# Converting six weight matrices with one DRAM-to-DRAM transfer each instead of tile by tile through SBUF

## The chip, the cores and the metric

The kernel runs on all 8 cores of one Trainium2 chip. Each core handles one of the eight sequences of the input and does the same work; the cores don't exchange data, and each converts its own copy of all weights. The metric is the device time of the slowest core in microseconds, lower is better.

## The reference

One transformer layer on an input of 8 x 4096 x 1024 float32. A modulation vector is made from `L0_c`, then an attention part and a gated feed-forward part are added to the stream:

```python
mod = (_silu(L0_c) @ L0_wmod).reshape(L0_c.shape[0], 6, 1, -1)
...
h = _layernorm(x, axis=-1) * (1 + ca) + sa
x = x + ga * _L0_attn_ref(h, ...)     # q, k, v, o: 1024x1024; fc: 4096x1024; proj: 1024x4096
h = _layernorm(x, axis=-1) * (1 + cb) + sb
x = x + gb * _L0_ffn_ref(h, w_gate, w_up, w_down)
```

`_L0_attn_ref` holds four projections, an attention over the 16 heads within each position, and a GELU MLP. `_L0_ffn_ref` uses weights quantized to -1, 0 and 1: each of gate, up and down (4 million elements each) is scaled by the mean of its absolute values, rounded and clipped:

```python
scale = 1.0 / jnp.clip(jnp.mean(jnp.abs(w)), 1e-05)
wq = jnp.clip(jnp.round(w * scale), -1.0, 1.0) / scale
```

All weights arrive as float32, and TensorE is to multiply in bfloat16.

## The kernel before

**Preparation.** The kernel first makes bfloat16 copies of all nine weight matrices in DRAM scratch tensors (`scr_q` ... `scr_d`), and then loads weights from these for every chunk. The preparation has three kinds of work.

- The modulation: 24 loads of 1024 KB of `wmod` into two buffers (`prefA`, `prefB`) on SP's queue (L252), each load waiting for the TensorE product that read its buffer before; 768 matmuls (L260); a copy of the result by VectorE (L271) and some small operations.
- Six casts, `prep_cast` (L309 to L321): q, k, v and o (1024 x 1024 each, 8 tiles of 128 x 1024), fc and proj (4 million elements each, 16 tiles of 128 x 2048; `fl` regroups the 128 columns of the tensor to rows of 2048). For each tile GpSimd issues a load from DRAM into the one buffer `prep_b` (L315), the DMA converting float32 to bfloat16 on the way, and SP issues the store from `prep_b` to the scratch tensor (L318). The load waits for the store before it, and the store for its load. `first_dep` chains the matrices one behind the other.
- Three quantizations, `prep_quant` (loads L332 and L382, reduction L336, conversions L385 and L389, stores L392): g, u and d, each read twice, once for the mean of its absolute values, once to convert. g begins when the modulation's product (`ev_mod_mm`) and the last cast are done, u after g, d after u. They use the same two buffers as wmod.

**Queues and dependencies.** The order on every engine is the order in which the operations are written. `Prog.op` turns dependencies into waits on semaphores. Every DMA of one of the two DMA queues (SP's "q", GpSimd's "g") alternates between two semaphores, and also waits until the semaphore's previous DMA has landed, so that at most two DMAs of a queue are in flight. A DMA instruction that waits holds back everything behind it on its engine:

```python
s = pool[self.dma_rr[dma] % len(pool)]
self.dma_rr[dma] += 1
deps = list(deps) + [(s, self.counts[s])]
```

SP's queue holds in this order: 11 loads of constants, the 24 loads of wmod, the 64 stores of the casts, the 48 stores of the quantizations, then for chunk 0 the load of x (L550) and the weight loads (`wload`, L421).

**Main part.** Eight chunks of 512 positions follow, one after the other: two layer norms, q, k, v in two slabs, attention, the o projection, fc and proj (weights from `scr_fc`, `scr_proj`), layer norm, gate and up, the requantization and down. Every weight load names the preparation of its matrix (`prep_done[...]`) as a dependency.

Of the kernel before, what the change touches and what calls it, by code (L numbers as in the profile page):

```python
# [15 lines left out]
D = 1024  # L16
H = 16
HD = 64
INNER = 4096
NCD = D // 128  # L20
NCI = INNER // 128
# [54 lines left out]
def build_nc(ttot=TTOT, chunk=CHUNK, slab=SLAB):  # L76
# [5 lines left out]
    p = Prog()  # L82

    dr = {}
# [44 lines left out]
    scr = {}  # L129
# [69 lines left out]
    prep_b = gfm[:, 0:2048]  # L199
# [24 lines left out]
    for nm in cb:  # L224
        p.op("sync", (lambda nm: lambda s: s.dma_start(out=cb[nm][:], in_=dr[nm]))(nm),
             dma="q")
    ev_const = [("dq0", p.counts["dq0"]), ("dq1", p.counts["dq1"])]

    if DBG and PHASE in (232, 99):
        ev_sent = p.op("vector", lambda v: v.memset(mmin[:, 0:128], 7.0), sig=True)  # L230
        p.op("sync", lambda s: s.dma_start(out=dbg["dbg_sbd"], in_=mmin[:, 0:128]),
             deps=[ev_sent], dma="q")
# [7 lines left out]
    for nm_, dst in (("qb_r", qbb), ("kb_r", kbb), ("vb_r", vbb)):  # L240
        ev_bb = p.op("gpsimd", (lambda nm_, dst: lambda g: g.dma_start(
            out=dst[:], in_=dr[nm_]))(nm_, dst), dma="g")
# [3 lines left out]
                   deps=ev_const, sig=True)  # L246
    ev_mod_mm = None
    wmod_hist = []
    for kc in range(8):
        for part in range(3):  # L250
            buf = prefA if (kc * 3 + part) % 2 == 0 else prefB
            evd = p.op("sync", (lambda kc, part, buf: lambda s: s.dma_start(  # L252
                out=buf[:], in_=dr["wmod"][128 * kc:128 * (kc + 1),
                                           2048 * part:2048 * (part + 1)]))(kc, part, buf),
                deps=(wmod_hist[-2] if len(wmod_hist) >= 2 else None,), dma="q")
            last = None
            for m in range(16):
# [3 lines left out]
                    out=bcp[0][:, mg:mg + 1], lhsT=buf[:, 128 * m:128 * (m + 1)],  # L261
                    rhs=siluc[:, kc:kc + 1],
                    start=(kc == 0 and mg == 0), stop=(kc == 7 and mg == 47)))(m, mg, kc, buf),
                    deps=[evd, ev_silu] + (bank_w("bc0") if (kc == 0 and mg == 0) else []),
                    sig=sig)
                if kc == 7 and mg == 47:
                    ev_mod_mm = last
            wmod_hist.append(last)
    if ev_mod_mm is None:
        ev_mod_mm = wmod_hist[-1]  # L270
    ev_mods = p.op("vector", lambda v: v.tensor_copy(out=mods[:], in_=bcp[0][:, 0:48]),  # L271
                   deps=(ev_mod_mm,), sig=True)
# [3 lines left out]
                  deps=(ev_mods,), sig=True)  # L276
    ev_cb1 = p.op("vector", lambda v: v.tensor_scalar(out=mods[:, 32:40], in0=mods[:, 32:40],
                                                      scalar1=1.0, scalar2=None, op0=ALU.add),
                  deps=(ev_mods,), sig=True)
    ev_g = ev_mods  # L280
    for col in (16, 40):
        ev_s0 = p.op("scalar", (lambda col: lambda s: s.activation(
            out=m8[:], in_=mods[:, col:col + 8], func=AF.Sign))(col),
            deps=(ev_g,), sig=True)
        ev_sq = p.op("vector", lambda v: v.scalar_tensor_tensor(
            out=trA[:, 0:8], in0=m8[:], scalar=1.0, in1=m8[:],
            op0=ALU.mult, op1=ALU.mult), deps=(ev_s0,), sig=True)
        ev_sq2 = p.op("vector", lambda v: v.tensor_scalar(
            out=trA[:, 0:8], in0=trA[:, 0:8], scalar1=-1.0, scalar2=1.0,
            op0=ALU.mult, op1=ALU.add), deps=(ev_sq,), sig=True)  # L290
        ev_sgn = p.op("vector", lambda v: v.tensor_tensor(
            out=m8[:], in0=m8[:], in1=trA[:, 0:8], op=ALU.add),
            deps=(ev_sq2,), sig=True)
        ev_a1 = p.op("vector", (lambda col: lambda v: v.scalar_tensor_tensor(
            out=trA[:, 0:8], in0=mods[:, col:col + 8], scalar=-1.0,
            in1=mods[:, col:col + 8], op0=ALU.mult, op1=ALU.max))(col),
            deps=(ev_g, ev_sgn), sig=True)
        ev_a2 = p.op("vector", lambda v: v.tensor_scalar(
            out=trA[:, 0:8], in0=trA[:, 0:8], scalar1=0.25, scalar2=None,
            op0=ALU.max), deps=(ev_a1,), sig=True)  # L300
        ev_g = p.op("vector", (lambda col: lambda v: v.tensor_tensor(
            out=mods[:, col:col + 8], in0=m8[:], in1=trA[:, 0:8],
            op=ALU.mult))(col), deps=(ev_a2, ev_sgn), sig=True)
    ev_mods_done = p.op("vector", lambda v: v.tensor_copy(out=m8[:], in_=mods[:, 0:8]),
                        deps=(ev_g, ev_ca1, ev_cb1), sig=True)

    prep_done = {}

    def prep_cast(src, dst, nrow128, ncols, first_dep=None):  # L309
        evo = None  # L310
        evi = first_dep
        for r in range(nrow128):
            for c0 in range(0, ncols, 2048):
                cw = min(2048, ncols - c0)
                evi = p.op("gpsimd", (lambda r, c0, cw: lambda g: g.dma_start(  # L315
                    out=prep_b[:, 0:cw], in_=src[128 * r:128 * (r + 1), c0:c0 + cw]))(r, c0, cw),
                    deps=(evo, evi), dma="g")
                evo = p.op("sync", (lambda r, c0, cw: lambda s: s.dma_start(  # L318
                    out=dst[128 * r:128 * (r + 1), c0:c0 + cw], in_=prep_b[:, 0:cw]))(r, c0, cw),
                    deps=(evi,), dma="q")  # L320
        return evo  # L321

    def prep_quant(src, dst, nrow128, ncols, sw_col, first_dep=None):
        nsl = nrow128 * (ncols // 2048)
# [54 lines left out]
        for r in range(nrow128):  # L379
            for c0 in range(0, ncols, 2048):  # L380
# [17 lines left out]

    fl = lambda apx: apx.rearrange("(r c) m -> r (c m)", c=16)
    prep_done["q"] = prep_cast(dr["qT"], scr["q"], NCD, D)  # L400
    prep_done["k"] = prep_cast(dr["kT"], scr["k"], NCD, D, first_dep=prep_done["q"])
    prep_done["v"] = prep_cast(dr["vT"], scr["v"], NCD, D, first_dep=prep_done["k"])
    prep_done["o"] = prep_cast(dr["oT"], scr["o"], NCD, D, first_dep=prep_done["v"])
    prep_done["fc"] = prep_cast(fl(dr["fcB"]), fl(scr["fc"]), NCI * D // 16 // 128, 2048,
                                first_dep=prep_done["o"])
    prep_done["proj"] = prep_cast(fl(dr["projB"]), fl(scr["proj"]),
                                  NCD * INNER // 16 // 128, 2048,
                                  first_dep=prep_done["fc"])
    prep_done["g"] = prep_quant(fl(dr["gB"]), fl(scr["g"]), NCI * D // 16 // 128, 2048, 0,
                                first_dep=[ev_mod_mm, prep_done["proj"]])  # L410
    prep_done["u"] = prep_quant(fl(dr["uB"]), fl(scr["u"]), NCI * D // 16 // 128, 2048, 1,
                                first_dep=[prep_done["g"]])
    prep_done["d"] = prep_quant(fl(dr["dB"]), fl(scr["d"]), NCD * INNER // 16 // 128, 2048, 2,
                                first_dep=[prep_done["u"]])
# [134 lines left out]
    for ci in range(nch):  # L549
        ev_x = p.op("sync", (lambda ci: lambda s: s.dma_start(  # L550
            out=xfm[:], in_=x_src[:, :, ci * chunk:(ci + 1) * chunk]))(ci),
            deps=[ev_store_prev] + ev_x_prev_readers, dma="q")
# [5 lines left out]
        if DBG and ci == 0:  # L558
            p.op("sync", lambda s: s.dma_start(out=dbg["dbg_mask"], in_=cb["mask128"][:]),
                 deps=ev_const, dma="q")  # L560
            p.op("sync", lambda s: s.dma_start(out=dbg["dbg_h"], in_=hfm[:]),
                 deps=evs_h + [("sV", p.counts["sV"]), ("sS", p.counts["sS"])], dma="q")
            p.op("sync", lambda s: s.dma_start(out=dbg["dbg_xn"], in_=mmin[:]),
                 deps=evs_xn, dma="q")
            p.op("sync", lambda s: s.dma_start(out=dbg["dbg_mods"], in_=mods[:]),
                 deps=[ev_mods_done], dma="q")

        if PHLE(1):
            ev_store_prev = p.op("sync", (lambda ci: lambda s: s.dma_start(
                out=out_dst[:, :, ci * chunk:(ci + 1) * chunk], in_=xfm[:]))(ci),  # L570
                deps=evs_xn, dma="q")
# [5 lines left out]
        for si in range(nslab):  # L577
# [4 lines left out]
            for TN in ("q", "k", "v"):  # L582
# [3 lines left out]
                for hb in range(4):  # L586
                    bank = pP[hb % 2]
                    ev_mm = None
                    for hs in range(4):
                        h = hb * 4 + hs  # L590
                        for kc in range(NCD):
# [3 lines left out]
                                             out=bank[0:64, hs * slab:(hs + 1) * slab],  # L595
# [46 lines left out]
            if DBG and ci == 0 and si == 0:  # L642
                p.op("sync", lambda s: s.dma_start(out=dbg["dbg_kq"], in_=khq[:]),
                     deps=dep_kh, dma="q")
# [723 lines left out]
```

How the kernel before makes its waits and increments, by code:

```python
            def run(eng):  # L1284
                waited = {}
                for emit, deps, incs in p.ops[eng_name]:
                    for (s, v) in deps:
                        if waited.get(s, 0) < v:
                            eng.wait_ge(sems[s], v)
                            waited[s] = v
                    inst = emit(eng)
                    if inst is not None:
                        for (s, amt) in incs:
                            inst.then_inc(sems[s], amt)
```

## Time and profile before

| | |
|---|---|
| median of 3 runs | 8901.75 us (8900.06 to 8910.51) |
| profiled execution | 8912.2 us |
| its span, core 4 (slowest) | 8910.7 us |
| spans of the 8 cores | 8828.5 to 8910.7 us |
| busy share of the span | TensorE 55%, VectorE 37%, ScalarE 9%, GpSimd 1% |
| mean granted TensorE clock, core 4 | 0.800 of full |
| first work of chunk 0 | 1313.4 us |

The span runs from the first to the last instruction of a core. Busy time is the time in which an engine executes; waiting and the issuing of DMAs don't count. The share of the DMA engines is a mean over the core's 16. The bytes of a DMA are those that it writes.

### The profile page before, as it was taken

To read this page: it belongs to the slowest core of one execution; us is meant where nothing else is said; L and a number is where in the kernel's file an instruction comes from. 1 tells how busy PE (TensorE), PEld (TensorE's weight loads), DVE (VectorE), ACT (ScalarE), POOL (GpSimd) and SP (SyncE) were. 2 spreads that over 40 slices of the span, in tenths; PEclk is the share of its full clock that TensorE was granted. 3 is DMA by queue.
4 is the path that set the end of the run, shared out by engine and by line. 5 is a ranking of instruction groups with operands and counts; after the bars stand their busy time and mean duration, and the time that the engine had idled before them with its cause. 6 is when DMAs were issued, how large, how long until landed. Compare 5 with 4: busy or idle time off the path is not lost.

```text
span 8910.7 us, 70916 instructions; the slowest of 8 cores (8828.5 to 8910.7 us)
## 1 busy us (share of the span) xinstructions
PE 4871.4 (55%) x23724; PEld 2394.2 (27%) x23948; DVE 3298.8 (37%) x6752; ACT 775.3 (9%) x1053; POOL 104.2 (1%) x167
## 2 busy tenths in 40 slices
PE   7000006566556665665656655665566656657566
PEld 7000003322332233222422233223322332214222
DVE  0003334335432543154324443354415432543244
ACT  0000001010101110110011010101011101100110
POOL 0001100000000000000000000000000000000000
PEclk9999997688668876887778867787688767877678
DMA  4355550133203330233113401332033202331133
GB/s 131 85 122 201 198 198 31 37 75 88 73 22 76 83 95 21 67 75 84 49 37 79 110 29 38 72 85 80 22 76 83 85 30 61 74 91 48 31 78 90
DMA packets 1051312, 692.64 MB, mean 78 GB/s; under 512 B 808144, under 2 KB 939344, under 8 KB 1035600
## 3 DMA queue, kind: packets, MB, share of 16 engines
q1 hardware_dynamic: 1027824, 562.26, 23.8%
q0 software_dynamic: 23136, 125.85, 5.1%
q8 instruction: 202, 3.31, 0.2%
q14 instruction: 150, 1.23, 0.0%
HBM read 646.09 MB, written 67.11 MB: 80 GB/s over the span
## 4 chain that ended last, share of the span: by engine, by line
PE 40%; DMA 26%; DVE 21%; issue 10%; ACT 2%; DVEq 1%; SPq 0%; ACTq 0%; POOLq 0%; POOL 0%
PE pA L594 5%; PE pB L594 4%; PE pB L1072 4%; PE pA L1066 3%; DVE sbd L685 3%; DMA wbigA<-scr_fc 2%; DMA wbigB<-scr_u 2%; PE pB L939 2%; PE pA L939 2%; DVE vtmp L1156 2%; DVE vtmp L497 2%; DMA wbigA<-scr_u 2%; PE pB L919 2%; DMA wbigB<-scr_g 2%; PE bcA L260 2%
## 5 line engine op out<-in xcount | busy, mean ns | idle before, releaser
L356 PE MATMUL bcB<-onecol_f,trA 128*1 128x1 f32 x6 | 0.6, 163 | 980.9 <-DVE prep_r L345 980.9
L948 DVE SCALAR_TENSOR_TENSOR vtmp<-pA,c_projb_f,afm 128x512 f32<-128x512 f32 x32 | 24.0, 751 | 1066.2 <-PE pA L939 1066.2
L447 PE MATMUL bcA<-amid,onescol_b 128*1 128x512 bf16 x256 | 102.9, 575 | 469.5 <-DVE amid L440 469.5
L1088 DVE TENSOR_TENSOR gu<-pB,gt 128x512 f32<-128x512 f32 x256 | 177.0, 692 | 445.7 <-PE pB L1072 445.7
L1066 PE MATMUL pA<-mmin,wbigB 128*128 128x512 bf16 x996 | 254.6, 391 | 147.0 <-DMA wbigB<-scr_g 87.5
L336 DVE TENSOR_REDUCE prep_r<-gfm 128x1 f32<-128x2048 f32 x48 | 109.6, 2286 | 604.5 <-DMA gfm<-gB 521.7
L1066 PE MATMUL pA<-mmin,wbigA 128*128 128x512 bf16 x996 | 253.0, 389 | 126.9 <-DMA wbigA<-scr_g 76.3
L1072 PE MATMUL pB<-mmin,wbigB 128*128 128x512 bf16 x1008 | 254.8, 395 | 72.7 <-DMA wbigB<-scr_u 71.3
L1072 PE MATMUL pB<-mmin,wbigA 128*128 128x512 bf16 x1008 | 254.1, 395 | 54.6 <-DMA wbigA<-scr_u 52.5
L356 PEld LDWEIGHTS bcB<-onecol_f,trA 128*1 128x1 f32 x6 | 0.3, 80 | 981.1 <-issue 981.1
L1086 ACT ACTIVATE sig<-gt 128x512 bf16<-128x512 f32 x256 | 161.1, 629 | 1141.3 <-DVE gt L1083 1141.2
L594 PE MATMUL pA<-mmin,wbigB 128*64 128x256 bf16 x1536 | 229.4, 294 | 38.9 <-ACT mmin L507 38.9
L594 PE MATMUL pA<-mmin,wbigA 128*64 128x256 bf16 x1536 | 226.7, 291 | 38.8 <-ACT mmin L507 38.8
L1083 DVE TENSOR_TENSOR gt<-pA,rsxg_t 128x512 f32<-128x512 f32 x256 | 176.6, 690 | 133.7 <-PE pA L1066 132.5
L1207 PE MATMUL pA<-gfm,wbigA 128*128 128x512 bf16 x504 | 164.2, 446 | 101.4 <-DVE gfm L1159 96.1
L1207 PE MATMUL pA<-gfm,wbigB 128*128 128x512 bf16 x504 | 164.1, 446 | 101.6 <-DVE gfm L1159 96.1
L469 ACT ACTIVATE row<-row,ceps 1x512 f32<-1x512 f32 x32 | 23.0, 720 | 2153.3 <-DVE row L464 2153.1
L594 PE MATMUL pB<-mmin,wbigB 128*64 128x256 bf16 x1536 | 203.7, 276 | 0.0
L594 PE MATMUL pB<-mmin,wbigA 128*64 128x256 bf16 x1536 | 203.7, 276 | 0.0
L626 DVE TENSOR_SCALAR gu<-gt 64x1024 bf16<-64x1024 bf16 x128 | 53.6, 419 | 401.6 <-ACT gt L622 401.6
L919 PE MATMUL pA<-mmin,wbigA 128*128 128x512 bf16 x504 | 146.1, 426 | 100.7 <-DMA wbigA<-scr_fc 63.9
L1156 DVE TENSOR_TENSOR vtmp<-gfm,sxb_t 128x512 int32<-128x512 bf16 x256 | 177.2, 692 | 56.3 <-ACT sxb_t L1129 30.4
(228 smaller groups left out, 9086.3 us busy)
## 6 DMA issues: line engine op xcount, KB each, us to landing
gfm<-gB POOLq DMA_DIRECT2D x32, 1024.0 KB, 6.4
gfm<-uB POOLq DMA_DIRECT2D x32, 1024.0 KB, 6.5
gfm<-dB POOLq DMA_DIRECT2D x32, 1024.0 KB, 6.4
wbigB<-scr_fc SPq DMA_DIRECT2D x128, 256.0 KB, 2.9
wbigA<-scr_fc SPq DMA_DIRECT2D x128, 256.0 KB, 2.9
wbigB<-scr_g SPq DMA_DIRECT2D x128, 256.0 KB, 2.9
wbigA<-scr_u SPq DMA_DIRECT2D x128, 256.0 KB, 2.9
wbigA<-scr_g SPq DMA_DIRECT2D x128, 256.0 KB, 2.9
```

The lines of the kernel that those rows point to most:

```text
L260: last = p.op("tensor", (lambda m, mg, kc, buf: lambda t: t.matmul(out=bcp[0][:, mg:mg + 1], lhsT=buf[:, 128 * m:128 * (m + 1)], rhs=siluc ...
L497: ev1 = p.op("vector", (lambda c, scl, vt: lambda v: v.scalar_tensor_tensor(out=vt[:], in0=src[:, c * chunk:(c + 1) * chunk], scalar=scl, ...
L594: (lambda h, hs, kc, wb, bank, t0, st: lambda t: t.matmul(out=bank[0:64, hs * slab:(hs + 1) * slab], lhsT=wb[:, kc * D + h * 64:kc * D + ( ...
L685: v.scalar_tensor_tensor(out=s_out, in0=s_in, scalar=1.0, in1=m_in, op0=ALU.mult, op1=ALU.mult))(s_in, m_in, s_out),
L919: ev_mm = p.op("tensor", (lambda oc, kc, wb, sl: lambda t: t.matmul(out=pslot(sl), lhsT=wb[:, kc * 128:(kc + 1) * 128], rhs=mmin[:, kc * c ...
L939: ev_mm = p.op("tensor", (lambda oc, kc, wb, sl: lambda t: t.matmul(out=pslot(sl), lhsT=wb[:, kc * 128:(kc + 1) * 128], rhs=gfm[:, kc * ch ...
L1066: ev_mg = p.op("tensor", (lambda oc, kc, wbg_, slg: lambda t: t.matmul(out=pslot(slg), lhsT=wbg_[:, kc * 128:(kc + 1) * 128], rhs=mmin[:, ...
L1072: ev_muu = p.op("tensor", (lambda oc, kc, wbu_, slu: lambda t: t.matmul(out=pslot(slu), lhsT=wbu_[:, kc * 128:(kc + 1) * 128], rhs=mmin[:, ...
L1083: ev_p1 = p.op("vector", (lambda slg, gt: lambda v: v.tensor_tensor(out=gt[:], in0=pslot(slg), in1=rsxg_t[:], op=ALU.mult))(slg, gt), deps ...
L1088: ev_p3 = p.op("vector", (lambda slu, gt, gu: lambda v: v.tensor_tensor(out=gu[:], in0=pslot(slu), in1=gt[:], op=ALU.mult))(slu, gt, gu), ...
L1156: ev_q1 = p.op("vector", (lambda oc: lambda v: v.tensor_tensor(out=qi[:], in0=gfm[:, oc * chunk:(oc + 1) * chunk], in1=sxb2_t[:], op=ALU.m ...
L1207: ev_mm = p.op("tensor", (lambda oc, kc, wb, sl: lambda t: t.matmul(out=pslot(sl), lhsT=wb[:, kc * 128:(kc + 1) * 128], rhs=gfm[:, kc * ch ...
```

## The change

`prep_cast` no longer goes through SBUF. It issues one DMA on GpSimd's queue from the whole float32 matrix to the whole scratch tensor, the DMA converting on the way. The six casts no longer depend on each other; fcB and projB are passed as declared (32768 x 128) and not regrouped. g's quantization no longer names the proj cast as a dependency, only the modulation's product. The rule of the two semaphores of a queue stays for all of them.

```diff
     def prep_cast(src, dst, nrow128, ncols, first_dep=None):
-        evo = None
-        evi = first_dep
-        for r in range(nrow128):
-            for c0 in range(0, ncols, 2048):
-                cw = min(2048, ncols - c0)
-                evi = p.op("gpsimd", (lambda r, c0, cw: lambda g: g.dma_start(
-                    out=prep_b[:, 0:cw], in_=src[128 * r:128 * (r + 1), c0:c0 + cw]))(r, c0, cw),
-                    deps=(evo, evi), dma="g")
-                evo = p.op("sync", (lambda r, c0, cw: lambda s: s.dma_start(
-                    out=dst[128 * r:128 * (r + 1), c0:c0 + cw], in_=prep_b[:, 0:cw]))(r, c0, cw),
-                    deps=(evi,), dma="q")
-        return evo
+        return p.op("gpsimd", lambda g: g.dma_start(out=dst, in_=src),
+                    deps=(first_dep,), dma="g")
...
     prep_done["q"] = prep_cast(dr["qT"], scr["q"], NCD, D)
-    prep_done["k"] = prep_cast(dr["kT"], scr["k"], NCD, D, first_dep=prep_done["q"])
-    prep_done["v"] = prep_cast(dr["vT"], scr["v"], NCD, D, first_dep=prep_done["k"])
-    prep_done["o"] = prep_cast(dr["oT"], scr["o"], NCD, D, first_dep=prep_done["v"])
-    prep_done["fc"] = prep_cast(fl(dr["fcB"]), fl(scr["fc"]), NCI * D // 16 // 128, 2048,
-                                first_dep=prep_done["o"])
-    prep_done["proj"] = prep_cast(fl(dr["projB"]), fl(scr["proj"]),
-                                  NCD * INNER // 16 // 128, 2048,
-                                  first_dep=prep_done["fc"])
+    prep_done["k"] = prep_cast(dr["kT"], scr["k"], NCD, D)
+    prep_done["v"] = prep_cast(dr["vT"], scr["v"], NCD, D)
+    prep_done["o"] = prep_cast(dr["oT"], scr["o"], NCD, D)
+    prep_done["fc"] = prep_cast(dr["fcB"], scr["fc"], NCI * D // 16 // 128, 2048)
+    prep_done["proj"] = prep_cast(dr["projB"], scr["proj"],
+                                  NCD * INNER // 16 // 128, 2048)
     prep_done["g"] = prep_quant(fl(dr["gB"]), fl(scr["g"]), NCI * D // 16 // 128, 2048, 0,
-                                first_dep=[ev_mod_mm, prep_done["proj"]])
+                                first_dep=[ev_mod_mm])
```

## Rows read from the trace of the kernel before

**Rows 1.** The page, part 2: busy tenths in 40 slices of the span.

```profile
PE   7000006566556665665656655665566656657566
...
DVE  0003334335432543154324443354415432543244
...
PEclk9999997688668876887778867787688767877678
DMA  4355550133203330233113401332033202331133
```

**Rows 2.** Windows of core 4: stretch, its length, busy us (x instructions) per engine, granted clock, DMA share, GB/s.

```profile
core 4: us, PE busy (x) PEld busy (x) DVE busy (x) ACT busy (x) POOL busy (x), PEclk, DMA share, GB/s
...
15.40:187.30 171.90, 164.10 (x768) 163.99 (x768) 0.05 (x1) 1.49 (x2) 0.53 (x1) 1.00 0.44 152
187.30:395.70 208.40, 0.00 (x0) 0.00 (x0) 2.61 (x16) 0.42 (x2) 15.82 (x30) 1.00 0.36 76
395.70:673.10 277.40, 0.00 (x0) 0.00 (x0) 0.00 (x0) 0.00 (x0) 16.92 (x33) 1.00 0.51 121
673.10:1302.90 629.80, 2.23 (x12) 1.83 (x12) 232.63 (x162) 0.00 (x0) 68.60 (x96) 1.00 0.56 199
1302.90:2255.90 953.00, 585.66 (x2868) 278.26 (x2896) 382.80 (x821) 97.80 (x132) 0.00 (x0) 0.79 0.26 65
2255.90:8910.70 6654.80, 4119.40 (x20076) 1950.14 (x20272) 2679.97 (x5747) 675.58 (x917) 0.00 (x0) 0.76 0.26 65
```

**Rows 3.** Timeline of GpSimd, SP and VectorE: start, us, instruction, wait before and releaser.

```profile
1.57 0.62 POOL L241 DMA_DIRECT2D qbb<-qb_r  x1 [0.88 <-POOLq L81]
...
5.77 0.54 POOL L315 DMA_DIRECT2D gfm<-qT  x1
181.28 0.53 POOL L315 DMA_DIRECT2D gfm<-qT  x1 [174.97 <-DMA scr_q<-gfm]
...
535.78 0.53 POOL L315 DMA_DIRECT2D gfm<-projB  x1 [7.95 <-DMA scr_fc<-gfm]
...
664.33 0.53 POOL L315 DMA_DIRECT2D gfm<-projB  x1 [8.05 <-DMA scr_proj<-gfm]
673.06 1.05 POOL L332 DMA_DIRECT2D gfm<-gB  x2 [8.21 <-DMA scr_proj<-gfm]
...
1.06 0.40 SPq L225 DMA_DIRECT2D c_ob_f<-ob_f  x1
...
14.30 0.33 SPq L225 DMA_DIRECT2D c_cfm<-cfm  x1
15.43 157.54 SPq L252 DMA_DIRECT2D gfm<-wmod  x24
173.12 51.91 SPq L318 DMA_DIRECT2D scr_q<-gfm  x8
...
541.27 128.87 SPq L318 DMA_DIRECT2D scr_proj<-gfm  x16
...
1302.85 0.38 SPq L550 DMA_DIRECT2D xfm<-x_fm  x1
...
187.25 0.21 DVE L271 COPY mods<-bcA 128x48 f32<-128x48 f32 x1 [185.33 <-PE bcA L260]
...
1313.37 2.29 DVE L440 CAST amid<-xfm 128x4096 bf16<-128x4096 f32 x1 [11.02 <-DMA xfm<-x_fm]
```

**Rows 4.** DMA queues in the casts of k, v and o, 230 to 395 us.

```profile
q0 software_dynamic: 3406, 6.19, 26.4%
q1 hardware_dynamic: 3456, 6.29, 10.1%
```

**Rows 5.** DMA queues in the casts of fcB and projB, 410 to 660 us.

```profile
q0 software_dynamic: 4147, 15.12, 36.0%
q1 hardware_dynamic: 4176, 15.21, 15.0%
```

**Rows 6.** Windows of cores 4 and 5, 686 to 690 us, during the gB loads.

```profile
686.00:690.00 4.00, 0.00 (x0) 0.00 (x0) 0.97 (x1) 0.00 (x0) 0.00 (x0) 1.00 0.98 379
...
core 5: us, PE busy (x) PEld busy (x) DVE busy (x) ACT busy (x) POOL busy (x), PEclk, DMA share, GB/s
686.00:690.00 4.00, 0.00 (x0) 0.00 (x0) 3.11 (x2) 0.00 (x0) 0.60 (x2) 1.00 0.32 68
```

**Rows 7.** DMA queues, 1700 to 1850 us, mostly loads of scr_fc.

```profile
q1 hardware_dynamic: 34320, 10.23, 29.9%
...
wbigA<-scr_fc SPq DMA_DIRECT2D x16, 256.0 KB, 2.9
```

## The prediction

> **What bounds the kernel now.** I read the page's forty slices first. TensorE is busy at the start, then has no digit above 0 until slice 7, while the DMA engines stand at 3 to 5 tenths: a stretch of some 1,100 us in which no engine sets the pace by its own work [rows 1]. The windows cut that stretch by what the code does in it [rows 2]. From 15.4 to 187.3 us TensorE multiplies wmod (164.1 of 171.9 us busy). From 187.3 to 673.1 us nothing computes: the six casts run. From 673.1 to 1302.9 us the three quantizations run, and then come eight chunks of about 951 us each ((8910.7 - 1302.9)/8).
>
> The timeline of the GpSimd and SP queues tells why the casts take so long [rows 3]. GpSimd issues the first qT tile at 5.77 us and the second at 181.28 us. The wait between them, 174.97 us, ends with the first store to scr_q, and that store stands in SP's queue behind all 24 wmod loads, the last of which waits for TensorE. From there on it is a strict alternation through one buffer: load a tile, store it, load the next, 6 to 7 us a pair for the 256 KB tiles and 8.6 us for the 512 KB ones (664.33 is the last of 16 projB tiles, the first was at 535.78: 128.55/15 = 8.57). The first gB load leaves at 673.06 us, released by the last scr_proj store. After it all is a chain: the quantizations, then at 1302.85 us the first x load in SP's queue, then at 1313.37 us the first work of chunk 0. So a microsecond taken from the 673.06 is a microsecond off the end, as long as the wmod product is not what the gB load waits for. It is done when VectorE copies it, at 187.25 us: that is the floor, and 673.1 - 187.3 = 486 us is the most that can be won.
>
> **The change, part by part.** It removes 64 loads on GpSimd's queue and 64 stores on SP's, with their waits, and adds six casting transfers from DRAM to DRAM. They have no dependency of their own. They keep the one that every DMA has, on the completion of the last but one of its queue, so two are in flight: q, v, fc share one semaphore, k, o, proj the other. They are issued from 5.8 us on, and nothing waits for SP any more. The order of gB moves: its first load waits for fc and for the wmod product, its second for proj. Behind these two stand all of GpSimd's quantization loads, and behind those VectorE. So what counts is one time, T, at which proj has landed and the wmod product is done. The saving is 673.1 - T; quantizations and chunks keep their durations, as their instructions and dependencies are the same.
>
> *Bytes.* The casts read 4 x 4.19 + 2 x 16.78 = 50.3 MB as float32 and write 25.2 MB as bfloat16 (the tiles show the written side: 8 x 256 KB and 16 x 512 KB). wmod is 24 x 1024 KB = 25.2 MB beside them.
>
> *The issuing.* 63 waits of some 8 us on GpSimd and as many on SP go. One DMA instruction holds GpSimd for 0.53 us at 128 rows and for 0.62 us at one row [rows 3]: a price per row can't be read from that, and six instructions cost some microseconds at most. Taken as 3 us, hidden behind the transfers before.
>
> *The transfers.* No row shows a DRAM-to-DRAM cast, so I bound it. What the 16 DMA engines do for the casts today, without the gaps, is share times duration [rows 2]: 0.36 x 208.4 + 0.51 x 277.4 = 75.0 + 141.5 = 216.5 us. Their wmod work is 0.44 x 171.9 = 75.6 us, and will now lie beside the casts instead of before them. With the engines kept full, T = 5.8 + 216.5 + 75.6 = 298 us, and 3 us of issue make it 301. This is what it costs if reading and writing take an engine as much as two transfers through SBUF do.
>
> The lower bounds: loads and stores come apart by queue, since the loads are GpSimd's (q0) and the stores SP's (q1). At 256 KB a load tile takes 0.264 x 165 x 16 = 697 engine-us for 3406/144 = 23.7 tiles, 29.5 each, or 230 ns for a row of 1024 elements [rows 4]. At 512 KB it is 0.360 x 250 x 16 = 1440 for 28.8 tiles, 50.0 each, or 391 ns for a row of 2048 [rows 5]; a store there takes 0.150 x 4000 / 29 = 20.7. If the write side hides wholly under the read side, the casts cost the loads alone: (32 x 29.5 + 32 x 50.0)/16 = 159 us, T = 5.8 + 75.6 + 159 = 240 us. If long rows also shed the fixed part (391 - 230 = 161 ns for 1024 elements, 69 ns fixed), it is 12,288 x 0.161/16 = 124 us and T = 205 us. All lie above the floor of 187. The upper ones are rivals, below.
>
> I take 301 us. The engines stood at a share of 0.98 and 379 GB/s only in bursts of a few microseconds, while a neighbouring core was at 68 GB/s in the same four [rows 6]; no row holds a burst rate for long, and now all eight cores cast at once, each writing to HBM half of what it reads. That speaks against the two low ends, which need 16 engines at read rate throughout. Saving: 673.1 - 301 = 372 us.
>
> The Trainium skill, HBM Reference, "Specifications (TRN2)", gives a core 358 GB/s when both cores of a pair stream. Casts and wmod move 50.3 + 25.2 + 25.2 = 100.7 MB over HBM, by that 281 us, so an estimate by the page is T = 287 us and a time of 8516 us. The row of 379 GB/s does not contradict it, since it lasts 4 us and the neighbour stood at 68; no run here shows a long stream yet.
>
> *What else could move.* The constants' loads on SP (1.06 to 14.30 us) and then wmod share the engines with the casts; each constant's load waits for an earlier one, so a few microseconds each, at most some 20 us, inside the range. The 64 stores no longer stand in SP's queue before the quantization's stores, which wait for VectorE anyway: nothing. TensorE's granted clock is 1.00 in every stretch before 1302.9 us and 0.76 to 0.79 after [rows 2]; it idles for over 100 us before chunk 0 in both kernels, so chunk 0 starts from the same state: nothing.
>
> *The sum.* The profiled execution took 8912.2 us (span 8910.7), 10 us over the median of the runs, 8901.75. Less 372 this is 8540 for that execution, and 8901.75 - 372 = 8530 us for a median.
>
> **The rivals.**
>
> *The write side hides* (T from 205 to 265 us). For it: one descriptor stream instead of two. Against it: HBM takes both sides at once. Time 8434 to 8494 us. Chance 0.22.
>
> *The wmod product becomes the late one.* The engines are shared between queues, and a wmod load may stand behind long cast rows; then TensorE waits for wmod until the casts are through. For it: wmod keeps TensorE busy 164.1 of 171.9 us [rows 2], so each load that comes later than its two buffers cover counts. Against: the DMA engines have 0.56 of their time free there. Worst case, the casts first and then the whole wmod stretch: 5.8 + 216.5 + 171.9 = 394 us, saving 279, time 8623 us. Chance 0.08.
>
> *Short rows.* fcB and projB are declared 128 columns wide; the old code regrouped them to rows of 2048 elements before the DMA, the new one hands them over as they are. If the rows stay 128 wide there are 65,536 of them. A row of 256 bytes costs 0.299 x 150 x 16 / 34,320 = 21 ns in the weight loads [rows 7], which would be cheap (86 us in all); with the cast's fixed part, 69 + 161/8 = 89 ns, it is 65,536 x 0.089/16 = 365 us, plus 59 for q, k, v and o: T = 5.8 + 75.6 + 365 + 59 = 506 us, saving 167, time 8735 us. Against it: both sides are contiguous, so nothing forces short rows. Chance 0.08.
>
> *One engine each (slower).* A contiguous block has no partition dimension, and if such a copy is not dealt out over the 16 engines, each of the two lanes runs at one engine's rate: 8 x 29.5 + 8 x 29.5 + 16 x 50.0 = 1272 us, T = 1278 us, 605 us later than now, time 9507 us. It decides from one engine: with two each, the lanes take 636 us, T = 642 us, and the time is still 31 us below the present one. For it: no row shows a DMA without a partition side. Against: the shares reach 0.98 of 16 engines in all others. Chance 0.05. The Trainium skill, DMA: Bandwidth & Descriptors, "Why a DMA increments its semaphore by 16 and not by 1", says that software can split a contiguous single-dimension pattern so that it sprays over the engines; by it this case would not come.
>
> *The casts stay as slow.* For T = 673 us the new transfers would have to read their 50.3 MB at 50.3/667 = 75 GB/s over 16 engines. The fit above gives one engine 4096 bytes in 161 ns, 25 GB/s, and the gB loads reach 379 GB/s on 16 [rows 6]; only some limit of the DRAM-to-DRAM path that no row shows could do it. No change. Chance 0.02.
>
> **How the numbers follow.** Main case 0.55, its own range T from 265 to 335 us, 8494 to 8564 us. Faster by over 0.2% (18 us, about what a measurement of this kernel can tell): 0.55 + 0.22 + 0.08 + 0.08 = 0.93. Same: 0.02. Slower: 0.05. The range reaches down to 8430, the bound where write side and fixed parts vanish, and up to 8640, over the late wmod product; short rows, one engine and no gain stay outside (0.15).
>
> **What the next profile would show.** The first gB load at about 301 us instead of 673.06, released by fc or proj. VectorE's copy of the wmod product not far past 187 us; if it comes at 300 or later, wmod is the late one. The DMA share from 6 us to T near 0.9 or higher: if it is at 1.0 and T near 240, the write side hides; if it is well below 0.9, the engines wait for memory. The quantizations at 630 us and the chunks at 951 us, unchanged. The forecast is wrong if the cast's packets are many and short, if a transfer lands on few engines, or if the quantization's pace depends on something that the casts left behind.

## The result, and the profile after

The changed kernel takes 8634.44 us (median of 9 runs, 8611.91 to 8709.33) against 8904.26 us before (10 runs): a ratio of 0.9707, 95% interval 0.9679 to 0.9736, some 270 us faster. The forecast was faster by 372 us. The direction held, but the median lies 104 us above the forecast of 8530, outside the likeliest case's own range (8494 to 8564), at the upper edge of the full one (8430 to 8640). By the ratio it is 8641 us (8616 to 8667) on the forecast's basis of 8901.75, just past that edge. The case that came is a rival, the late wmod product, which had 8623 us and a chance of 0.08.

The page of the profiled execution (8664.66 us, span 8662.9 on core 0), part 2. Against [rows 1] the empty stretch of TensorE has moved: its 7 tenths come one slice later, and the DMA share of the first slice is 9.

```profile
PE   0700065666566575665566655665666656657566
...
DMA  9555501333033311332033211340133303331134
```

The windows of core 0: stretch, length, busy us (x instructions) per engine, granted clock, DMA share, GB/s.

```profile
5.70:183.00 177.30, 0.00 (x0) 0.00 (x0) 0.00 (x0) 0.00 (x0) 3.13 (x7) 1.00 1.01 110
183.00:242.00 59.00, 0.00 (x0) 0.00 (x0) 0.00 (x0) 1.49 (x2) 0.00 (x0) 1.00 0.95 113
242.00:408.60 166.60, 163.97 (x768) 163.91 (x768) 0.40 (x3) 0.21 (x1) 0.03 (x1) 1.00 0.43 146
408.60:1038.10 629.50, 2.23 (x12) 1.83 (x12) 234.94 (x176) 0.21 (x1) 68.63 (x96) 1.00 0.56 199
1038.10:8662.90 7624.80, 4744.64 (x23168) 2237.97 (x23168) 3066.40 (x6568) 773.32 (x1049) 0.00 (x0) 0.76 0.26 64
```

Against [rows 2]: until 242 us the DMA engines are full and TensorE does nothing at all. The wmod product then takes 166.6 us at a DMA share of 0.43, as it did before at 0.44. The quantizations take 629.5 us (629.8) and the chunks (8662.9 - 1038.1)/8 = 953 us each (951). So everything that the forecast left alone did stay, and the whole error lies ahead of 408.6 us.

The timelines of GpSimd, SP and VectorE: start, us, instruction, wait before and its releaser.

```profile
5.71 0.51 POOL L310 DMA_DIRECT2D scr_q<-qT  x1
...
86.50 0.55 POOL L310 DMA_DIRECT2D scr_proj<-projB  x1 [18.13 <-DMA scr_o<-oT]
408.57 1.08 POOL L322 DMA_DIRECT2D gfm<-gB  x2 [321.52 <-PE bcA L260]
...
6.77 0.33 SPq L225 DMA_DIRECT2D c_ln2b_f<-ln2b_f  x1
...
144.35 0.33 SPq L225 DMA_DIRECT2D c_cfm<-cfm  x1
183.00 211.74 SPq L252 DMA_DIRECT2D gfm<-wmod  x24
...
1038.13 0.38 SPq L538 DMA_DIRECT2D xfm<-x_fm  x1
...
408.09 0.21 DVE L271 COPY mods<-bcA 128x48 f32<-128x48 f32 x1 [406.18 <-PE bcA L260]
```

GpSimd issues its six casts as forecast and waits for nothing of SP's. SP's queue does not run as forecast: c_cfm, issued at 14.30 us in [rows 3], goes out at 144.35 us, and wmod begins at 183.00 us instead of 15.43. The first gB load leaves at 408.57 us, released by the wmod product and not by a cast. Its time against 673.06 is a saving of 264.5 us, which is the measured one (some 270 us) within the scatter of the runs. The DMA queues from 6 to 242 us (name, kind: packets, MB written, share; below, KB and us from issue to landing):

```profile
q0 software_dynamic: 896, 25.17, 97.2%
q1 hardware_dynamic: 1051, 0.99, 2.2%
...
scr_proj<-projB POOLq DMA_DIRECT2D x1, 8192.0 KB, 155.4
...
c_cfm<-cfm SPq DMA_DIRECT2D x1, 4.0 KB, 81.9
```

A transfer of 128 rows shows 144 packets in the kernel before, one of a single row 32. Without 16 for each of the six casts and 32 for vbb, the 896 packets are 768 rows, and 25.17 MB over 768 are 32,768 bytes written: the rows are 64 KB read and 32 KB written, eight times longer than any row of the casts before. A constant of 4 KB takes 82 us to land.

### The profile page after: what moved, and what is told of

Same layout as the page of the kernel before. It is cut to its first block, busy times and chain, and to the rows that moved or that the text cites. A ratio compares the mean times of both kernels' runs of the same rounds, so it can differ in the third digit from the quotient of the medians.

```text
span 8662.9 us, 70774 instructions; the slowest of 8 cores (8566.8 to 8662.9 us)
## 1 busy us (share of the span) xinstructions
PE 4910.8 (57%) x23948; PEld 2403.7 (28%) x23948; DVE 3302.5 (38%) x6752; ACT 775.2 (9%) x1053; POOL 73.6 (1%) x109
## 3 DMA queue, kind: packets, MB, share of 16 engines
q8 instruction: 202, 3.31, 0.2%
## 4 chain that ended last, share of the span: by engine, by line
PE 41%; DMA 22%; DVE 21%; issue 10%; another core or an unknown queue 3%; ACT 2%; DVEq 1%; SPq 0%; ACTq 0%; POOL 0%; POOLq 0%
PE pA L582 5%; PE pB L582 5%; PE pB L1060 3%; PE pA L1054 3%; DVE sbd L673 3%; PE pB L927 2%; DMA wbigA<-scr_u 2%; DVE vtmp L1144 2%; DMA wbigA<-scr_fc 2%; DMA wbigB<-scr_fc 2%; DMA wbigA<-scr_g 2%; DMA wbigB<-scr_u 2%; DVE vtmp L485 2%; PE bcA L260 2%
## 5 line engine op out<-in xcount | busy, mean ns | idle before, releaser
L1054 PE MATMUL pA<-mmin,wbigB 128*128 128x512 bf16 x1024 | 255.5, 388 | 140.6 <-DMA wbigB<-scr_g 93.7
L260 PE MATMUL bcA<-siluc,gfm 128*128 128x1 f32 x768 | 164.0, 352 | 244.0 <-DMA gfm<-wmod 244.0
L260 PEld LDWEIGHTS bcA<-siluc,gfm 128*128 128x128 f32 x768 | 163.9, 333 | 244.0 <-issue 244.0
L907 PE MATMUL pA<-mmin,wbigB 128*128 128x512 bf16 x512 | 144.0, 419 | 96.5 <-DMA wbigB<-scr_fc 61.5
```

The costliest lines, as they stand in the source:

```text
L260: last = p.op("tensor", (lambda m, mg, kc, buf: lambda t: t.matmul(out=bcp[0][:, mg:mg + 1], lhsT=buf[:, 128 * m:128 * (m + 1)], rhs=siluc ...
L907: ev_mm = p.op("tensor", (lambda oc, kc, wb, sl: lambda t: t.matmul(out=pslot(sl), lhsT=wb[:, kc * 128:(kc + 1) * 128], rhs=mmin[:, kc * c ...
L1054: ev_mg = p.op("tensor", (lambda oc, kc, wbg_, slg: lambda t: t.matmul(out=pslot(slg), lhsT=wbg_[:, kc * 128:(kc + 1) * 128], rhs=mmin[:, ...
```

## The experiments

Theory A: a row of 64 KB occupies a DMA engine for 4.8 us, and a packet of SP's queue comes through only between such rows; so wmod starves until the casts are done. "MB/ms" in the expectations is GB/s. T is again the time at which the gB load leaves that waited for the last of casts and product. Single executions of the changed kernel scatter from 8612 to 8709 us, so the experiments with one run are read by T and not by their time.

**Rows of 8 KB.**

```diff
-        return p.op("gpsimd", lambda g: g.dma_start(out=dst, in_=src),
+        return p.op("gpsimd", lambda g: g.dma_start(out=dst, in_=src, max_dma_last_dim=8192),
```

> The changed kernel with the six casts cut into rows of 2048 elements (8 KB read, 4 KB written) instead of 16,384. Theory A (each cast row of 64 KB holds a DMA engine for 4.8 us, and the constants and wmod loads of SP's queue get one short packet in between): the first wmod load goes out before 30 us instead of at 183 us, wmod shares the engines with the casts, the first gB load leaves at about 310 us (236 us of casts + 76 us of wmod) instead of 408.6, time about 100 us below the changed kernel, 8535. Rival B (GpSimd's queue is served first, or the memory path is full, whatever the row length): the first wmod load still after 150 us and gB at about 408 us, time 8634.

Measured: 8556.44 us, ratio 0.9617 (0.959 to 0.9644), clear of the changed kernel's interval. T is 331 us. SP's and GpSimd's timelines:

```profile
35.84 0.33 SPq L225 DMA_DIRECT2D c_cfm<-cfm  x1
45.77 266.35 SPq L252 DMA_DIRECT2D gfm<-wmod  x24
...
330.93 1.08 POOL L322 DMA_DIRECT2D gfm<-gB  x2 [224.93 <-PE bcA L260]
```

Theory A holds: wmod goes out at 46 us, and its product is done 8 us after the last cast lands (104.99 + 217.7 = 322.7 us). The first load was 16 us later than expected and T 21 us, with a DMA share of 0.93 until wmod goes out and 0.97 from there to T: the engines are all but full, and the two kinds of work take more than the expected 236 + 76 = 312 us together.

**The first cast behind the constants, rows of 64 KB.**

```diff
-    prep_done["q"] = prep_cast(dr["qT"], scr["q"], NCD, D)
+    prep_done["q"] = prep_cast(dr["qT"], scr["q"], NCD, D, first_dep=ev_const)
```

> The changed kernel, rows of 64 KB, but the first cast waits for all constants (and those behind it with it). Theory A: the constants cost what they cost before (wmod goes out at 15 us), but each wmod load takes some 60 us while the casts run (two in flight, so some 8 of 24 are in by 256 us), the other 16 follow at 7.2 us each: gB at about 370 us instead of 408.6, time about 8595. Rival C (only the constants' lateness matters): wmod runs as fast beside the casts as alone, gB when the casts end, about 255 us, time 8480.

Measured: T = 392.13 us, 8618.64 us (one run). Constants and wmod are on time (wmod at 14.17 us), yet T falls by 16 us only, with the casts starting 9 us later. DMA queues, 20 to 240 us:

```profile
q0 software_dynamic: 768, 22.54, 88.0%
q1 hardware_dynamic: 790, 5.73, 12.8%
...
gfm<-wmod SPq DMA_DIRECT2D x6, 1024.0 KB, 75.0
```

Six wmod loads in 220 us, each 75 us to landing: the constants' lateness was a small part, rival C falls, and the loads starve still more than expected (eight).

**The first cast behind the wmod product**, with `first_dep=[ev_mod_mm]` in the same place.

> The changed kernel, but the first cast waits for the wmod product: nothing overlaps. If the casts alone take the DMA engines 236 us for 50.3 MB read, in whatever company, gB leaves at 187 + 236 = 423 us, time about 15 us above the changed kernel, 8650: all that the early start of the casts brings in the changed kernel is 15 us. If the casts were slowed by the constants and wmod beside them, it is earlier: at 216 us (the load and store work of before) 403 us.

Measured: T = 420.20 us, 8661.92 us (one run). The casts, alone from 185.98 us, take 234 us. In the changed kernel they took 236 with wmod waiting beside them. So the early start brought the changed kernel 12 us of T; the other 253 come from the end of the alternation. DMA queues of this kernel, 200 to 410 us:

```profile
q0 software_dynamic: 770, 22.61, 99.2%
```

0.992 x 210 x 16 engine-us for 22.61 MB / 32,768 = 690 rows is 4.83 us a row, 13.6 GB/s an engine and 215 GB/s read for 16. The share is full: the casts leave the engines no idle time in which something else could lie.

**Both: rows of 8 KB behind the constants.**

> Rows of 8 KB and the first cast behind the constants. Theory A: as e1, within 10 us (gB at about 310 us), since short rows already let the constants through. Rival: if the constants are still late in e1, this is earlier than e1 by that lateness.

Measured: T = 331.20 us, 8561.88 us (one run); with the first experiment's 330.93 within 1 us, as expected. Here the product is done at 292.57 us and proj is the last. Windows of core 4:

```profile
15.40:290.00 274.60, 164.38 (x758) 163.18 (x758) 0.00 (x0) 1.02 (x2) 4.50 (x6) 1.00 1.00 167
295.00:328.00 33.00, 0.00 (x0) 0.00 (x0) 1.19 (x7) 0.03 (x1) 0.00 (x0) 1.00 1.00 109
```

With the engines full from 15 us on, the casts (50.3 MB read and 25.2 written, 75.5 MB) and 25.2 MB of wmod need 317 us: 318 GB/s of DRAM reads and writes. Only more bandwidth, or another place for the casts, would give more. The rows of 8 KB in the second stretch take 1.00 x 33 x 16 / 875 = 0.60 us, the same 13.6 GB/s an engine as those of 64 KB.

**What bounds the cast: a plain copy and converting loads.**

```diff
+    ev_x1 = p.op("gpsimd", lambda g: g.dma_start(out=scrx, in_=dr["fcB"]),
+                 deps=[prep_done["proj"], prep_done["fc"]], dma="g")
+    xs = dr["fcB"].rearrange("(t r c) m -> t r (c m)", r=128, c=64)
+    for t_ in range(4):
+        ev_x1 = p.op("gpsimd", (lambda t_: lambda g: g.dma_start(
+            out=gfm[:, 0:8192], in_=xs[t_]))(t_), deps=[ev_x1], dma="g")
```

> A measurement, with extra work that the reference has not: casts behind the wmod product, then one plain copy of fcB (16.8 MB read, 16.8 MB written, DRAM to DRAM, no conversion), then four converting loads of 4.2 MB from fcB into SBUF. If DRAM to DRAM is bound by the bytes read and written together (the cast: 219 read + 110 written = 329 MB/ms), the copy takes 33.6/329 = 102 us. If the read side or the engine's handling of a row sets the cast's rate (13.7 MB/ms an engine), it takes 77 us. If the conversion is what costs, it takes less, down to 16.8/400 = 42 us. A converting load of 4.2 MB into SBUF takes 19 us if the conversion costs, 11 us if the write to DRAM does. gB leaves at about 560 us.

```profile
417.13 0.55 POOL L398 DMA_DIRECT2D scr_x<-fcB  x1 [150.49 <-DMA scr_proj<-projB]
519.84 0.55 POOL L402 DMA_DIRECT2D gfm<-fcB  x1 [102.17 <-DMA scr_x<-fcB]
535.05 0.54 POOL L402 DMA_DIRECT2D gfm<-fcB  x1 [14.65 <-DMA gfm<-fcB]
```

One run, 8790.33 us with the extra work. The copy takes 102.2 us. Bytes read and written together gave 102 (33.6 MB at the expectation's 329 GB/s) or 104 (at the 323 GB/s that the casts alone ran at: 75.5 MB in 234 us); a limit on the read side gave 77, one on the conversion less. Measured, it is 328 GB/s. A converting load of 4.2 MB into SBUF takes 14.2 us from issue to landing, 295 GB/s with its start and end in it. Neither the conversion nor an engine's read side is the limit.

**Reading alone, and SBUF alone.**

```diff
+    for t_ in range(8):
+        d_ = [prep_done["fc"], prep_done["proj"]] if t_ == 0 else []
+        hx.append(p.op("gpsimd", (lambda t_: lambda g: g.dma_start(
+            out=(gA if t_ % 2 == 0 else gB_), in_=xs[t_]))(t_), deps=d_, dma="g"))
...
+    for t_ in range(4):
+        ev_x1 = p.op("gpsimd", lambda g: g.dma_start(out=gB_, in_=gA),
+                     deps=[hx[-1], hx[-2]], dma="g")
```

> A measurement, with extra work that the reference has not: casts behind the wmod product; then eight plain loads of 2.1 MB of fcB from DRAM into SBUF, two in flight (16.8 MB, rows of 16 KB, no conversion), then four copies of 2.1 MB from one half of SBUF to the other, one at a time. The casts, the plain DRAM-to-DRAM copy and the casts through SBUF all ran at 313 to 328 MB/ms of DRAM reads and writes together. If this is what DRAM gives a core with all eight at work, reading alone is no faster: 16.8/0.325 = 52 us for the eight loads, and a copy inside SBUF, which leaves DRAM out, takes 5 to 6 us plus a fixed 2. If reads alone reach the 379 MB/ms of the bursts or more, 44 us or less, it is the mix of reading and writing that costs. If the copy inside SBUF takes over 10 us (2.1 MB read and 2.1 MB written), the engines themselves are the limit for whatever is read and written.

```profile
412.17 1.09 POOL L403 DMA_DIRECT2D gfm<-fcB  x2 [147.20 <-DMA scr_proj<-projB]
423.00 0.53 POOL L403 DMA_DIRECT2D gfm<-fcB  x1 [9.74 <-DMA gfm<-fcB]
...
456.34 0.53 POOL L403 DMA_DIRECT2D gfm<-fcB  x1 [7.10 <-DMA gfm<-fcB]
466.91 0.53 POOL L407 DMA_DIRECT2D gfm<-gfm  x1 [10.04 <-DMA gfm<-fcB]
475.85 0.53 POOL L407 DMA_DIRECT2D gfm<-gfm  x1 [8.41 <-DMA gfm<-gfm]
```

One run, 8675.34 us with the extra work. Eight loads from 412.17 to 466.91 us are 16.8 MB in 54.7 us, 307 GB/s with start and end in it: reads alone are no faster than the mix. A copy inside SBUF lands in 8.4 us, at least 250 GB/s read and 250 written at once, with its start and end in it, where the copy from DRAM to DRAM had 164 and 164. So what bounds the casts in rows of 8 and 64 KB is not what the engines can move: the DRAM side gives a core about 320 GB/s, reads and writes together, while all eight are at it. For reads alone an engine limit at the same height is not excluded by these loads, but the 379 GB/s of [rows 6], in 4 us with the neighbour at 68, speak against it and for a limit that the cores share. Whether the DRAM side means the memory or the way to it, these runs don't separate; in all of them the eight cores are at it together.

**The casts through four SBUF buffers**, stores on ScalarE's queue.

```diff
+            b = stage_i[0] % 4
+            stage_i[0] += 1
+            buf = gfm[:, 2048 * b:2048 * b + ncols]
+            evi = p.op("gpsimd", (lambda r, buf: lambda g: g.dma_start(
+                out=buf, in_=src[128 * r:128 * (r + 1), :]))(r, buf),
+                deps=[stage_free[b]], dma="g")
+            evo = p.op("scalar", (lambda r, buf: lambda s: s.dma_start(
+                out=dst[128 * r:128 * (r + 1), :], in_=buf))(r, buf),
+                deps=[evi], dma="s")
```

> The casts again tile by tile through SBUF, but with four staging buffers and the stores on ScalarE's queue with semaphores of their own, so that neither wmod nor the one buffer holds them up: 64 loads and 64 stores as in the kernel before, issued from 5 us on beside wmod. By the forecast's price (216 us of engine work, 76 us of wmod) gB leaves at about 300 us, some 30 us before the direct casts with rows of 8 KB (331): the detour through SBUF costs the engines less than the direct cast. Rival: two transfers cost more than one, gB at 360 us or later.

Measured: T = 442.90 us, 8662.59 us (one run). As a test of the overlap it failed by its own design: the first store sits in ScalarE's queue behind an activation that waits for the wmod product, and goes out at 193.33 us. The 442.90 us therefore say nothing for or against the forecast of 300. What the run does show is the price. ScalarE's and GpSimd's timelines:

```profile
191.31 0.21 ACT L285 ACTIVATE m<-mods 128x8 f32<-128x8 f32 x1 [169.38 <-DVE mods L274]
...
193.33 14.82 ACTq L324 DMA_DIRECT2D scr_q<-gfm  x8
...
286.14 74.42 ACTq L324 DMA_DIRECT2D scr_fc<-gfm  x16
...
279.11 1.15 POOL L321 DMA_DIRECT2D gfm<-fcB  x2 [8.75 <-DMA scr_o<-gfm]
...
442.90 1.05 POOL L342 DMA_DIRECT2D gfm<-gB  x2 [12.91 <-DMA scr_proj<-gfm]
```

From the first fc load, issued at 279.11 us, to the end, fc and proj take 442.9 - 279.1 = 164 us, which is 307 GB/s for 50.3 MB read and written; the direct casts' rate gives the same bytes 50.3/0.323 = 156 us. (Counted from the first store, at 286.14, it is 157 us, but by then four of the 32 loads are out.) With four buffers the detour through SBUF costs some 5% more than the direct form: what the change removed was in the main the alternation, not a transfer.

**The casts of fc and proj behind the quantizations**, rows of 8 KB: `prep_done["fc"]` and `prep_done["proj"]` are set after `prep_done["d"]`.

> Rows of 8 KB, the first cast behind the constants, and the casts of fc and proj issued behind the last quantization load, to run beside chunk 0, which needs them only some 400 us after its start. Then only q, k, v and o (4.19 MB read each, 19 us each) lie beside wmod. Theory A with the casts' measured rate (219 MB/ms): the wmod product is done at about 210 us, gB leaves then, the x load of chunk 0 at about 840 us. Chunk 0's first loads share the engines with 157 us of casts; its x load is 64 packets an engine, each behind a cast row of 0.6 us: some 40 us late. Time about 8903 - 463 + 40 = 8480. Rival: the casts of fc and proj are in the way of the weight loads of chunk 0 all along and give back their 157 us: 8600.

**The same, with rows of 64 KB for these two.**

> As the kernel with the casts of fc and proj behind the quantizations, but those two with rows of 64 KB. Theory A: the x load of chunk 0 (64 packets an engine) gets one packet in per one or two cast rows of 4.8 us, so it is held up until the casts are through, about 150 us: chunk 0 starts some 110 us later than with rows of 8 KB, time about 8590. Rival B (row length doesn't matter): as with rows of 8 KB, 8480.

Measured: 8530.74 us, ratio 0.9595 (0.9546 to 0.9645), and 8638.08 us (one run). In both the first gB load leaves at 227.5 us, where about 210 was expected. VectorE's first work of chunk 0 in the one and in the other:

```profile
919.21 2.29 DVE L428 CAST amid<-xfm 128x4096 bf16<-128x4096 f32 x1 [63.08 <-DMA xfm<-x_fm]
```

```profile
1014.17 2.29 DVE L431 CAST amid<-xfm 128x4096 bf16<-128x4096 f32 x1 [119.67 <-DMA xfm<-x_fm]
```

Rows of 64 KB start chunk 0 95 us later than rows of 8 KB, as theory A has it, at another place and against other loads. But the rows of 8 KB cost more than expected as well: the x load takes 62.5 us and the first q load 96.7 us instead of 9 and 12 (medians of the kernel before), and the time is 50 us over the expected 8480. Chunk 0 takes 1025 us from its x load to the next, 72 more than before.

**The casts of fc and proj beside the attention of chunk 0.**

```diff
             ev_qkv_last = ev_kh["v"]
+            if ci == 0:
+                nm_ = ("fc", "proj")[si]
+                prep_done[nm_] = cast8k(dr[nm_ + "B"], scr[nm_], ev_kh["v"])
```

> Rows of 8 KB; q, k, v and o beside wmod, as in the kernel with the casts of fc and proj behind the quantizations; but the cast of fc now waits for the end of the v projection of slab 0 of chunk 0, and that of proj for the same of slab 1: both lie beside an attention stretch of about 120 us each in which the DMA share is 0.04 to 0.11. Theory: the casts' price is one of place alone, so here it is hidden: gB leaves at 227 us as there, the x load of chunk 0 lands in 10 us instead of 62, and chunk 0 loses at most 10 us. Time 8903 - (673 - 227) = 8457, up to 8470. Rival: the casts slow something else in chunk 0 (the weight loads at the end of the attention), time as with the casts right behind the quantizations, 8530.

**The same, with rows of 2 KB for q, k, v and o** (`max_dma_last_dim=2048`).

> As the kernel with the casts of fc and proj in the attention, but q, k, v and o with rows of 512 elements (2 KB read, 1 KB written). Theory A: a wmod load waits for shorter rows, so the wmod product comes between 190 and 227 us, at about 205, and the time is some 20 us lower, 8440; the four casts take 77 us of DRAM traffic as before and land a little later. Rival (the forecast's fixed part of 69 ns a row holds for such a cast): a row takes 69 + 80 = 149 ns as if the rate were memory's anyway, no change in the casts' own time. If a row of 2 KB takes more than 150 ns at a full queue, the fixed part is real, and the casts land later than 160 us.

Measured: 8462.1 us, ratio 0.9512 (0.9468 to 0.9555), and 8470.08 us, ratio 0.9509 (0.9478 to 0.9539). The first is as expected: GpSimd issues the two casts at 994.76 and 1149.12 us, they land in 78.6 and 73.9 us, and the x load in 13.5 us. Chunk 0 takes 951 us in the mean of the eight cores (948 before). It is the fastest kind found, some 170 us below the changed kernel. The second missed: the two can't be told apart, and its gB leaves at 242.03 us, released by the wmod product, not earlier than the 227.27 us of the first. The DMA queues of the first and then of the second, each at 20 to 75 and at 80 to 125 us:

```profile
q0 software_dynamic: 1079, 4.30, 60.1%
q1 hardware_dynamic: 695, 5.04, 40.4%
...
q0 software_dynamic: 870, 3.50, 62.4%
q1 hardware_dynamic: 559, 4.06, 38.1%
```

```profile
q0 software_dynamic: 3254, 3.31, 71.6%
q1 hardware_dynamic: 661, 4.82, 27.1%
...
q0 software_dynamic: 3722, 3.78, 81.6%
q1 hardware_dynamic: 452, 3.33, 20.8%
```

A row of 2 KB takes 0.716 x 55 x 16 / (3.31 MB/1024) = 0.195 us in the first stretch and 0.159 us in the second (10.5 and 12.9 GB/s an engine); over all eight cores it is 0.159 to 0.198. A row of 8 KB at the same place takes 0.50 and 0.53 us, a quarter of it 0.13. So the short row does cost extra. It is over the 150 ns that the expectation named as the sign of a fixed part, but its other sign, casts that land later than 160 us, did not come: the last lands at 140 us, against 128 with rows of 8 KB. How much of the extra is the forecast's 69 ns the run doesn't isolate. DRAM traffic, reads and writes, falls with it: (3 x 3.31 + 4.82)/55 us = 268 GB/s in the first stretch, against 326 with rows of 8 KB, at a DMA share that is just as full (over cores and stretches 259 to 326 against 316 to 336).

And wmod gets less, not more: 4.82 MB against 5.04 and 3.33 against 4.06. A wmod row (8 KB) comes through after 5.5 and 9.1 cast rows of 2 KB in the two stretches (5.5 to 10.6 over the cores, 11 to 22 KB), after 1.4 to 2.0 rows of 8 KB (11 to 16 KB), and after 1.0 of 64 KB in the kernel with the constants first. So an engine passes some 11 to 22 KB of the casts for each wmod row, or a whole row if that is longer; this is read from counts, and what makes an engine change queues no run here shows. Below 8 KB nothing is won.

## Why the prediction missed

- *What counts is one time, T, and the saving is 673.1 - T.* Right: 264.5 us by the profile, about 270 by the medians.
- *Quantizations and chunks keep their durations.* Right: 629.5 against 629.8, 953 against 951 us.
- *GpSimd's queue and the issue cost.* Right: six instructions of 0.50 to 0.56 us.
- *The casts take the DMA engines 216.5 us.* Mis-sized by 20: 236 us from 5.7 to 242, 234 alone. The forecast took the engines' work of the old form and had the mechanism wrong: not an engine's handling, but the DRAM side's 320 GB/s is the limit. The busy shares of the old kernel (0.36 and 0.51) did not show it: by them fc and proj are 141.5 us of work, and the same loads and stores through four buffers took 164 us with the engines full.
- *"Their wmod work is 0.44 x 171.9 = 75.6 us, and will now lie beside the casts instead of before them."* This is the step that failed. Nothing of the wmod product lay beside the casts (TensorE's first matmul starts at 244.01 us); it followed them with its full 166.6 us, which is 91 us more than the 75.6 of the sum. 20 + 91 - 3 (issue, which cost nothing) = 108, the whole of 408.6 - 301. The experiment with rows of 8 KB and nothing else takes 78 us of this off T again.
- *"each constant's load waits for an earlier one, so a few microseconds each, at most some 20 us, inside the range"*: c_cfm was 130 us late. In T this cost 16 us (the run with the constants first), because wmod starved in any case.
- *The rival of the late product* had the right mechanism and 394 us for its worst case; the measured 408.6 is past that by the 20 us of the casts, less the 5 by which the wmod stretch was shorter (166.6 against 171.9). Its chance was too low. The argument against it, that the DMA engines have 0.56 of their time free in the wmod stretch, counted time and not turns: beside casts that fill the engines with rows of 4.8 us there is no free time, and wmod gets one row in for each of theirs.
- *The rival of short rows* was the wrong way round. The contiguous matrices became rows of 64 KB, 768 in all, and that is what did the harm. *One engine each*, *the casts stay as slow* and *the write side hides* fell too: the share was 1.0 over 16 engines, and reads and writes add up.
- *The estimate by the Trainium skill* (HBM Reference, "Specifications (TRN2)": 358 GB/s a core with both of a pair streaming) gave T = 287. The runs show 307 to 328 GB/s a core (casts, plain copy, casts and wmod, casts through SBUF, reads) in rows of 8 KB and more, with all eight cores at work: the page's kind of limit is the one that binds, some tenth below its figure, and the measurement decides. Even so it is right only for work that overlaps.

## What to carry to other kernels

A transfer moved off the critical path still has its place among the others: ask what shares the DMA engines with it and how long its rows are, since a queue of loads beside a cast with rows of 64 KB gets one row in per 4.8 us on each engine. Cap the row, here at 8 KB, and not lower: at 2 KB the rows cost extra and the loads beside them gained nothing. A direct DRAM-to-DRAM form saves waits, hardly bandwidth; count the bytes read and written in DRAM by all that is to overlap, and divide by what a full stretch shows. Once the engines are full, look for a stretch where the DMA share is low, and put the transfer there.

## What had not been expected of the hardware

- One core's DRAM reads and writes together came to about 320 GB/s with all eight cores at it: casts 323, plain copy 328, casts and wmod 318, reads alone 307 with their start and end, casts through SBUF 307.
- A contiguous cast from DRAM to DRAM went out in rows of 64 KB read. Between 64 and 8 KB row length made no difference to its own rate (13.6 GB/s an engine, alone), and a large one to others. At 2 KB, beside wmod, it ran at 10.3 to 12.9 GB/s an engine, where rows of 8 KB had 14.5 to 16.8.
- Of two queues on the same engines, the one with small packets gets its turn after a whole long row, or after some 11 to 22 KB of shorter ones: a 4 KB constant took 82 us to land.
